# State space layer of a decoder: convolutions one slot behind their input products with four buffers, the decays of four tiles in one slot, a convolution tile first

## The reference

```python
zxbcdt = u @ W_in.T
z, xBC, dt = jnp.split(zxbcdt, [D_INNER, D_INNER + CONV_DIM], axis=-1)
conv = conv_b
for k in range(D_CONV):                       # 4 taps
    conv = conv + xp[:, k:k + l, :] * conv_w[:, k]
xBC = jax.nn.silu(conv)                       # x (128), B (128), C (512)
dt = jax.nn.softplus(dt + dt_bias)
A = -jnp.exp(A_log)
y = _chunked_scan(xh, dt, A, Bh, Ch, D)       # decays exp(segment sums of dt*A), weighted by C.B and dt
y = y * jax.nn.silu(z)
rstd = jax.lax.rsqrt(jnp.mean(yg * yg, axis=-1, keepdims=True) + EPS)
y = (yg * rstd).reshape(b, l, D_INNER) * norm_weight
return y @ W_out.T                            # then x = layernorm(x + y)
```

## Time and profile before

| | us |
|---|---|
| median of 3 runs (lowest, highest) | 1364.76 (1362.14, 1367.31) |
| the profiled execution: its time, its span | 1364.1, 1362.3 |
| busy in the span: PE, DVE, ACT, POOL | 1153.6, 774.0, 587.5, 439.6 |
| the state space layer, from the end of the block before to the next layer's first work | 701 to 920.5 |

### The profile page before, as it was taken

How to read it: one execution, slowest core, us unless ns; L and a number is a source line. 1 busy time by engine, 2 the same in 40 slices (tenths; PEclk the granted TensorE clock), 3 DMA queues, 4 the chain that set the end, 5 groups by cost and what they waited for, 6 DMA issues and landing times. The chain is left out here.

```text
span 1362.3 us, 21103 instructions
## 1 busy us (share of the span) xinstructions
PE 1153.6 (85%) x7532; PEld 679.7 (50%) x7532; DVE 774.0 (57%) x1524; ACT 587.5 (43%) x1221; POOL 439.6 (32%) x689
## 2 busy tenths in 40 slices
PE   5788774888998759899847888879999899999997
PEld 2555552444544325577512444457778433545454
DVE  1566667788888341233445667763555545555565
ACT  1455540476767721233245546526666242222120
POOL 4677745145444326333223224342111100000001
PEclk9799985799999969899968999998999889999999
DMA  5434723465655202233321200000000000000000
GB/s 161 143 93 150 239 83 90 115 142 140 150 147 129 51 25 86 90 106 108 121 90 31 102 0 1 1 1 1 2 2 2 24 1 1 4 12 5 12 5 28
DMA packets 72015, 91.65 MB, mean 67 GB/s; under 512 B 12232, under 2 KB 61024, under 8 KB 71104
## 3 DMA queue, kind: packets, MB, share of 16 engines
q1 hardware_dynamic: 67494, 80.65, 21.2%
q0 software_dynamic: 3408, 9.34, 1.9%
q10 hardware_dynamic: 1010, 0.31, 0.1%
HBM read 55.37 MB, written 29.17 MB: 62 GB/s over the span
## 5 line engine op out<-in xcount | busy, mean ns | idle before, releaser
L808 DVE TENSOR_REDUCE b_nm<-b_s 128x4 f32<-128x1024 f32 x128 | 150.7, 1209 | 29.5 <-PE b_s L899 29.4
L855 ACT ACTIVATE b_pr<-b_s 128x512 f32<-128x512 f32 x256 | 142.9, 603 | 56.6 <-PE b_s L918 56.6
L918 PE MATMUL b_s<-b_qs,b_ks 75*128 75x256 bf16 x512 | 90.1, 279 | 25.2 <-ACT b_pr L855 20.8
L899 PE MATMUL b_s<-b_ks,b_qs 72*128 72x256 bf16 x512 | 85.4, 294 | 16.2 <-DMA b_qs<-qparts 12.1
L2367 POOL TENSOR_SCALAR f_rstd<-f_mv 128x1 f32<-128x1 f32 x16 | 3.8, 239 | 269.4 <-DVE f_mv L2506 269.3
L2451 DVE TENSOR_TENSOR f_prod<-f_sg,f_kept 128x512 f32<-128x512 f32 (+1 forms) x48 | 33.2, 691 | 97.9 <-ACT f_kept L2396 95.0
L1727 DVE SCALAR_TENSOR_TENSOR d_acc<-d_pad,d_cw,d_acc 128x512 f32<-128x512 f32 x72 | 60.4, 844 | 45.4 <-ACT d_acc L1652 43.7
L2576 PE MATMUL fps_h<-residT,w_f_w 128*128 128x512 f32 x176 | 83.5, 615 | 2.5 <-DVE f_inner L2488 2.5
L1840 PE MATMUL dps_ip<-residT,d_win 128*128 128x512 f32 x160 | 77.3, 617 | 5.2 <-ACT d_acc L1652 3.2
L318 POOL TENSOR_TENSOR a_nrm<-a_ss,phalf 128x20 f32<-128x20 f32 x16 | 58.5, 3655 | 52.5 <-DVE a_ss L446 52.5
L899 PEld LDWEIGHTS b_s<-b_ks,b_qs 72*128 72x128 bf16 x512 | 46.2, 102 | 53.1 <-issue 20.3
(11 more groups left out here) (400 smaller groups left out, 2682.7 us busy)
## 6 DMA issues: line engine op xcount, KB each, us to landing
kparts<-a_cparts SPq DMA_DIRECT2D x48, 192.0 KB, 2.8
b_ks<-kparts SPq DMA_DIRECT2D x32, 288.0 KB
b_qs<-qparts SPq DMA_DIRECT2D x96, 96.0 KB
b_nd<-b_os SPq DMA_DIRECT2D x64, 128.0 KB, 3.1
xrows<-in_c_fill SPq DMA_DIRECT2D x13, 387.0 KB, 4.7
c_xrow<-xrows SPq DMA_DIRECT2D x39, 129.0 KB
c_back<-routed SPq DMA_DIRECT2D x8, 512.0 KB, 5.1
qparts<-b_xp SPq DMA_DIRECT2D x48, 64.0 KB, 2.7
```

Of the source, the lines that this page charges most:

```text
L808: dve.tensor_reduce(nm[s % 2][:, 4 * n:4 * n + 4].rearrange("p (g h) -> p g h", h=2), s1[step % 2][:], AX.X, ALU.max, negate=True).then_in ...
L855: act.activation(pr[g % 8][:], s2[g % 2][:], ACT.Exp, scale=SCALE).then_inc(s2_out, 1)
L899: ins = pe.matmul(s1[step % 2][:, g % 2, qh, :], qs[s % 3][0:ROWS, g, qh * P:(qh + 1) * P], ks[s % 3][0:ROWS, g, :], start=True, stop=True)
L918: ins = pe.matmul(s2[g % 2][:, lh, :], ks[x % 3][0:ROWS + 3, g, lh * P:(lh + 1) * P], qs[x % 3][0:ROWS + 3, g, :], start=True, stop=True)
```

## The change

The convolutions of a slot's jobs, and their Silus, stand one slot later than their products (`later_convolved`); `d_pad` and `d_acc` have four buffers. The weighting of `d_es` by `d_dtm` (`time`) now comes ahead of that by C.B (`weigh`) and stands at the end of the slot before. POOL makes `d_dam` from a new `d_dta` (dt times A) instead of from `d_dtm`, and both of them after the two norm steps of its slot. Decays and segment sums of four tiles stand in slots 3, 7 and 11 (and four in the lead), between the slot's other jobs. The deal of jobs is new, and chunk 0 begins with a convolution block. `d_win` comes in two transfers, the gates' part of its own.

```diff
-    lead = [("in", 0, m) for m in (6, 7, 8, 9, 0, 1, 2, 3, 4, 5)] + [("mixed", 0, 0)]
-    dealt = {-1: lead}
-    for c in range(1, NCHUNK):
-        first = 0 if c == 1 else 4 * c - 5
-        row = [("in", c, m) for m in (0, 1, 2, 6, 3, 7, 4, 8, 5, 9)] + [("mixed", c, 0)]
-        split = ((0, 4), (4, 8), (8, 11)) if c == 1 else ((0, 2), (2, 5), (5, 8), (8, 11))
+    dealt = {-1: [("in", 0, m) for m in (0, 6, 1, 7, 2, 8, 3, 9, 4, 5)] + [("mixed", 0, 0), ("in", 1, 0), ("in", 1, 1)],
+             0: [("in", 1, 2), ("in", 1, 3)], 1: [("in", 1, 4), ("in", 1, 6), ("in", 1, 5)],
+             2: [("in", 1, 7), ("in", 1, 8), ("in", 1, 9), ("mixed", 1, 0)]}
+    for c in range(2, NCHUNK):
+        at = TPC * (c - 1)
+        for slot, row in ((at - 2, (0, 1)), (at - 1, (2, 3)), (at, (4, 6, 5)), (at + 1, (7, 8)), (at + 2, (9,))):
+            dealt[slot] = dealt.get(slot, []) + [("in", c, m) for m in row]
+        dealt[at + 2].append(("mixed", c, 0))
...
+    def later_convolved(s):
+        return [n for n in slot_jobs.get(s - 1, []) if jobs[n] in nth and (s > 0 or jobs[n][1] > 0)]
...
-        pad, acc = many(2, "pad", [P, SPC, CW - 1 + T]), many(2, "acc", [P, SPC, T])
+        pad, acc = many(4, "pad", [P, SPC, CW - 1 + T]), many(4, "acc", [P, SPC, T])
...
 POOL, each slot
-                    if live(s + 4):
-                        decays(s + 4)
                     if live(s - 1):
                         rms_power(s - 1)
                     if live(s - 3):
                         variance_power(s - 3)
+                    if live(s + 3):
+                        weight_steps(s + 3)
+                    if live(s + 4):
+                        decay_steps(s + 4)
...
 ACT, each slot
-                    if todo:
-                        work(todo[0])
-                    if s % 2 == 0 and live(s + 2):
-                        decay(s + 2)
-                        decay(s + 3)
-                    for n in todo[1:]:
-                        work(n)
+                    batch = range(s + 1, s + 1 + TPC) if s % TPC == TPC - 1 and live(s + 1) else range(0)
+                    for at in range(max(len(todo), len(batch))):
+                        if at < len(batch):
+                            decay(batch[at])
+                        if at < len(todo):
+                            evacuate(todo[at])
                     if live(s):
                         square(s)
+                    for n in later_convolved(s):
+                        activate(jobs[n])
...
 DVE, each slot
+                    todo = later_convolved(s)
                     if live(s):
                         weigh(s)
                     if live(s - 3):
                         add_up(s - 3)
-                    for n in todo[:2]:
-                        convolve(n)
                     if live(s):
                         gated(s)
                     if live(s - 3):
                         statistics(s - 3)
+                    for n in todo[:1]:
+                        convolve(n)
                     if live(s - 1):
                         mean_square(s - 1)
-                    for n in todo[2:]:
+                    for n in todo[1:]:
                         convolve(n)
+                    if live(s + 1):
+                        time(s + 1)
...
 PE, each slot
-                    if s % 2 == 0 and live(s + 2):
-                        segments(s + 2)
-                    if todo:
-                        fill(todo[0])
+                    batch = list(range(s + 1, s + 1 + TPC)) if s % TPC == TPC - 1 and live(s + 1) else []
+                    for q in batch[:1]:
+                        segments(q)
+                    for n in todo[:1]:
+                        fill(n)
                     if live(s):
                         mix(s)
+                    for q in batch[1:2]:
+                        segments(q)
                     if live(s + 1):
                         products(s + 1)
-                    if s % 2 == 0 and live(s + 3):
-                        segments(s + 3)
+                    for n in todo[1:2]:
+                        fill(n)
+                    for q in batch[2:3]:
+                        segments(q)
                     if live(s - 1):
                         square_sums(s - 1)
-                    for n in todo[1:2]:
-                        fill(n)
                     if live(s - 2):
                         put_out(s - 2)
+                    for q in batch[3:]:
+                        segments(q)
                     for n in todo[2:]:
                         fill(n)
```

More of the change, by code:

```diff
@@ L1572, in _ @@
                     sp.dma_start(dst[:], io[src]).then_inc(dt_const, 16)
+                for dst, src in conv_consts:
+                    sp.dma_start(dst[:], src).then_inc(conv_const, 16)
+                sp.dma_start(wz[:], io["d_win"][:, :, XT * P:]).then_inc(gate_const, 16)
                 for dst, src in consts:
@@ L1691, in _ @@
                 act.activation(e[:], ab[:], ACT.Exp, scale=-1.0).then_inc(e_done, 1)
-                act.wait_ge(const, 16 * len(consts))
-                act.wait_ge(padded, 2)
-                for n in slot_jobs[-1]:
-                    work(n)
-                    if n == ZT - 1:
-                        for g in range(G):
-                            ins = act.activation(wout[:, g, :], wout[:, g, :], ACT.Copy, scale=nw[:, g:g + 1])
-                        ins.then_inc(wout_done, 1)
-                decay(0)
@@ L1701, in _ @@
-                decay(1)
+                act.wait_ge(conv_const, 16 * len(conv_consts))
+                act.wait_ge(padded, 4)
+                own = [n for n in slot_jobs[-1] if jobs[n][1] == 0]
+                for n in own[:6]:
+                    evacuate(n)
+                activate(("in", 0, 0))
+                act.wait_ge(const, 16 * len(consts))
+                for g in range(G):
+                    ins = act.activation(wout[:, g, :], wout[:, g, :], ACT.Copy, scale=nw[:, g:g + 1])
@@ new lines, in _ @@
+                ins.then_inc(wout_done, 1)
+                evacuate(own[6])
+                evacuate(own[7])
+                activate(("in", 0, 1))
+                evacuate(own[8])
+                activate(("in", 0, 2))
+                evacuate(own[9])
+                for q in range(4):
+                    decay(q)
+                activate(("in", 0, 3))
+                evacuate(own[10])
+                activate(("in", 0, 4))
+                activate(("in", 0, 5))
+                for n in slot_jobs[-1][len(own):]:
+                    evacuate(n)
@@ L1857, in segments @@
                         pe.wait_ge(seg_out, q)
[L1858 removed]
+                    pe.matmul(seg_ps[:], later[:], dam[q % 4][:], start=True, stop=True).then_inc(seg_full, 1)
                 def products(q):
@@ L1916, in _ @@
                 ins.then_inc(dt_full, 1)
+                own = [n for n in slot_jobs[-1] if jobs[n][1] == 0]
+                for n in own[:10]:
+                    fill(n)
                 pe.wait_ge(const, 16 * len(consts))
-                for n in slot_jobs[-1]:
+                for q in range(4):
+                    segments(q)
+                fill(own[10])
+                for n in slot_jobs[-1][len(own):]:
                     fill(n)
-                segments(0)
-                segments(1)
                 products(0)
```

101 lines of the change are left out of this document (53 added, 48 removed).

## The result

Over 12 runs of each kernel, the changed one has a median of 1370.80 us (1360.95 to 1374.11) and the kernel before 1363.74 (1359.80 to 1368.23, one run at 1468.25 aside). The ratio is 1.0041, 95% interval 1.0024 to 1.0057: slower by 0.4%, some 3 to 8 us. The forecast was 1361.

What follows compares the result with a forecast made beforehand. PE was taken as near its limit in the middle windows, often late behind DVE. Lead -2.0, windows -5.5, -1.0, -4.7 and +9.7 sum to -3.5 us from 1364.1: 1360.6, median 1361, own range 1357 to 1366, whole range 1351 to 1369.

Steps and rivals of the forecast that it cites:

- the step on the decays: Slots 3, 7 and 11: four decays add PE waits for the exponential and `d_dam`, plus 1.5 us of half clock.
- lead, against before: Before mix(0): four changes end between -3.9 and +0.4 us, depending on the clock; -2.0 taken.
- mix(0) to mix(3): First three slots: 8.0 and 8.5 set by DVE, then 14.6 on PE; 31.1 us, 5.5 less than before.
- mix(3) to mix(7): Slots 3 to 6: 15.9 + 9.7 + 9.6 + 11.5 = 46.7 us, 1.0 less than before.
- mix(7) to mix(11): Slots 7 to 10: 15.3 + 10.2 + 9.6 + 6.1 = 41.2 us, 4.7 less than before.
- mix(11) to mix(15): Slots 11 to 14: 15.6, three slots of 4.8, and 1.5 for half clock; 31.5 us, 9.7 more than before.
- The chain of slot 3: Slot 3: fourth segment sums wait for `d_dam` behind the same slot's mean square; PE stands 3.9 us, mix(4) at 15.9.
- batching the decays makes it slower: Rival: each batch slot's two PE gaps bring low clock costing 4.5 us; 1371.5, possibly past 1375; chance 0.14.
- the last rival: The change doesn't do what it says: DVE's convolutions still bind PE, six slots lose 1.6 more; 1370, chance 0.13.
- POOL's chain: On POOL, from the start of DVE's mean square to the end of `d_dam`: 5.28 us.
- DVE's loop: DVE's slot with two convolutions: 4.5 + 1.15 + 1.56 + 1.95 = 9.2 us, plus 0.4 for overlap with POOL.
- the low end: Lead: if the clock falls earlier, five products and segment sums run at half speed, about 4 us; gain 0.

Runs made afterwards that it cites:

- e3_warm: The changed kernel with nine unused matrix products on PE ahead of the fourth segment sums in slots 3, 7 and 11; layer 222.5 us, ratio 0.9945.
- e6: The changed kernel with decays in pairs and the product into `d_dam` first in POOL's slot; layer 202.6 us, ratio 0.9862 to the kernel before.
- e11: The changed kernel with decays in pairs, the `d_dam` product first on POOL and 15 unused PE products in the lead; layer 200.0 us, ratio 0.9813.
- e5_decay_before_weight: The changed kernel with POOL's last two products exchanged, `d_dam` ahead of `d_dtm`, both behind the norm steps; layer 224.7 us, ratio 1.0004.
- e9_pairs_same_slot: The changed kernel with decays in pairs and convolutions and Silus back in the slot of their own input products; layer 228.9 us, ratio 1.0058.
- e10: The changed kernel with decays in pairs and 15 unused PE products between the lead's four segment sums; layer 201.3 us, ratio 0.9858.
- e2_pairs: The changed kernel with decays and segment sums back in pairs in even slots, POOL's order as changed; layer 204.5 us, ratio 0.9843.
- e1_pool_first: The changed kernel with the product into `d_dam` put first in POOL's slot, ahead of the norm steps; layer 208.5 us, ratio 0.9891.

## Why the prediction was wrong

The mechanism was right at nearly every step, and the sum was wrong: -3.5 forecast, +8.0 in the layer. The price that failed is the clock, in the step on the decays ("With PE so idle I expect a stretch at half clock ... I take 1.5"): half clock came behind all three gaps and cost some 9.7 us, 8 of the 11.5 that are missing. The lead is 2.1 more of them, DVE's first slots 1.4.

| stretch | forecast | measured |
|---|---|---|
| lead, against before | -2.0 | +0.1 |
| mix(0) to mix(3) | 31.1 | 32.54 |
| mix(3) to mix(7) | 46.7 | 48.69 |
| mix(7) to mix(11) | 41.2 | 43.97 |
| mix(11) to mix(15) | 31.5 | 34.97 |

- **The chain of slot 3, in its parts.** Forecast from mix(3)'s start: mean square at 7.9, `d_dam` at 13.2, PE's wait 3.9, segment sums and product 2.7, mix(4) at 15.9. Measured: 7.7, 13.7, 4.3, 5.4, 19.1. The place, the releaser and the length of the wait were right. Of the 3.2 us that are missing, 2.7 is half clock behind the gap and 0.5 POOL. Slot 7 has the same: 15.3 forecast, 18.3 measured, 2.6 of it clock.
- **The half clock.** I counted 1.5 us, once, in slot 12. It came after each of the three gaps: 2.7 and 2.6 in slots 3 and 7 (e3_warm gives back 2.6 and 2.6), and a stretch of 13.30 us at 0.50 with 11.52 of PE busy in slots 11 and 12. There the forecast for slot 11 was missed by 1.3 (15.6, measured 16.9) and for slot 12 by 3.6 (4.8, measured 8.4, and 5.3 at full clock in e6 and e11, so 3.1 of clock). Together some 9.7 us in place of 1.5; the 5.2 of slots 3 and 7 are isolated by e3_warm, the rest is read from rows. I had taken one row at 805.8 as evidence that a gap of 3.3 us keeps the clock; e5_decay_before_weight and e9_pairs_same_slot show that gaps of the same length lose it. The rival "batching the decays makes it slower" had this mechanism at 4.5 us a slot; its chance of 0.14 was too low. Its sum was wrong as well: 13.5 - 1.5 + 2 is 14.0 over the forecast, 1375, and not the 10.5 and 1371.5 that stand there. So the measured 1370.8, close to that figure, doesn't confirm it. The 1370 of the last rival is luck too: DVE's convolutions don't bind PE any more.
- **POOL's chain.** 6.04 us from the mean square to the end of `d_dam` in slot 3, not 5.28. The forecast moved the large products away from the convolutions, and the norm steps took their place there. The groups of POOL in the slots show it, before and after (line, count, busy us, mean ns, idle before):

```profile
L1597 POOL TENSOR_TENSOR d_rs<-d_ms,mhalf 128x4 f32<-128x4 f32 x15 | 15.5, 1033 | 65.2 <-DVE d_ms L1782 65.2
L1606 POOL TENSOR_TENSOR d_rstd<-d_rstd,mhalf 128x1 f32<-128x1 f32 x12 | 6.9, 578 | 1.0
```

```profile
L1607 POOL TENSOR_TENSOR d_rs<-d_ms,mhalf 128x4 f32<-128x4 f32 x15 | 21.0, 1398 | 106.2 <-DVE d_ms L1809 106.2
L1616 POOL TENSOR_TENSOR d_rstd<-d_rstd,mhalf 128x1 f32<-128x1 f32 x12 | 8.7, 723 | 1.0
```

- **DVE's loop.** Slot 1 took 9.9 us for 8.5: its convolution beside POOL's norm step and `d_dtm` 3.20, and `time` beside `d_dam` 1.53 for 0.69. Priced at 0.4, this was 1.7. Slots 5 and 9 took 8.3 for 9.6. DVE's loop had the forecast length there (from the end of one tile's weighting at 798.69 to the next at 808.28, 9.6), but DVE came out of slot 4, which PE bound, 1.3 us ahead. Slot 8 was 1.0 longer than forecast: PE waited 0.92 for ACT to take a block out.
- **The lead.** -2.0 forecast, +0.1 measured. The half clock between the exponentials came as the low end said, and one more stretch at the lead's first products, which other executions of the same lead don't have. Without either it is -1.6 (e10, with its added products).
- **Right:** PE's wait on DVE (12.2 to 5.4), DVE's wait for ACT gone, the fourth segment sums behind `d_dam` in all three slots (4.3, 4.3, 3.5), mix(12) behind the turn (a wait of 1.8 on ACT), 9 table loads.

The median moved by 7.1 us and the ratio says 5.6, for 8.0 in the one profiled layer. Where the expected gain went can be told, to some us, from the layer times: 219.0 before, +9.9 for the rest of the change (e9_pairs_same_slot, 228.9), -24.4 for the lag (e2_pairs, 204.5), +22.5 for the batch of four (227.0). By the ratios the three steps are +8, -29 and +27. The batch took its part by the three waits of 12.1 us in all and the clock behind them, most of which the place of one call on POOL gives back (18.5 us, e1_pool_first).

## What to carry to other kernels

A batch that a slow engine has to feed puts a gap into PE's work, and the gap is paid twice: as idle time and, behind most such gaps here, as products at half clock. When such a gap is forecast, price the work behind it at half clock, each time, unless several rows show the opposite. An item that a later slot needs and that depends on nothing of this slot stands first on its in-order engine, not behind items that do; and two parts of one change are worth a 2 by 2 table, as a good one (with the lag and pairs the kernel is 1.6% faster than before) can hide behind a bad one.

## What the runs showed of the hardware

- The granted clock fell to 0.50 behind PE gaps of 3.49, 4.28 and 4.30 us in the changed kernel, of 2.48, 3.27 and 3.29 in e5 and of 3.32 in e9. It stayed at 1.00 over one of 3.32 in the kernel before, where on the other hand it fell at 776 with no gap over 1.4 us in the 10 us ahead. Behind the same gap of 2.42 us ahead of mix(1) it stayed in the changed kernel (slot 1: 9.94 us) and fell in e1_pool_first (11.59), though both have the same work for PE there. The length of the gap alone does not tell it. The Trainium skill, "TensorE: Matmul & The Clock Gate", section "What's actually happening", says that the slow clock is the default and activity releases it; the traces agree, as in slots 3 and 7 the nine products without use of e3_warm kept the clock where only waiting had lost it.
- Some of POOL's small operations slow down beside DVE: the norm's power on 128x4 took 1.45 us beside a convolution, with a mean of 1033 ns before and 1398 after, and that on 128x1 0.86 with a mean of 578 and 723. The two smallest did not (means of 190 and 228 ns before, 191 and 229 after). And DVE's 128x512 product `time` took 1.53 us beside `d_dam`, 0.69 alone, and `d_dam` 1.49 for 1.05. The Trainium skill, "SBUF — State Buffer", section "SBUF: two separate sides", says that GpSimd and a DVE operation with two inputs from SBUF share a port pair which one of them holds for a whole instruction. The traces agree in direction: both sides grew.
